# Second attention: weighing with the value slices stationary in four column groups

## The chip, the core and the metric

The kernel runs on one core of a Trainium2 chip. The metric is device time in microseconds (us) of one execution. The core has TensorE (PE: matmuls, with weight loads shown apart as PEld), VectorE (DVE), ScalarE (ACT), GpSimd (POOL) and SyncE (SP), each with its own queue, which it works through in order.

## What is computed

32 batches of 128 tokens with 128 features go through four parts, each added to its input: an attention of 16 heads of 8, a mixture of 8 experts (two for each token, with a capacity), a second attention of 16 heads of 64, and a mixture of 16 experts (one for each token) beside a shared one. The change lies in the second attention:

```python
q = (x @ w_q).reshape(B, SQ, N_HEADS, D_HEAD)        # 16 heads of 64
k = (cond @ w_k).reshape(B, SKV, N_HEADS, D_HEAD)
v = (cond @ w_v).reshape(B, SKV, N_HEADS, D_HEAD)
attn = jnp.einsum('bqhd,bkhd->bhqk', q, k) * scale
attn = jax.nn.softmax(attn, axis=-1)
out = jnp.einsum('bhqk,bkhd->bqhd', attn, v).reshape(B, SQ, N_HEADS * D_HEAD)
return out @ w_out + b_out
```

## The kernel before

One batch of 128 queries and 128 keys is one step of the second attention; `attention` in the TensorE block writes the order of a step by hand, and the blocks of the other engines have the same loop `for b in range(1, LAST)` (30 steps, b = 1 to 30) with their parts. What is in flight is of several batches: step b has the scores of b, the coarse product (for the row maxima) and the values of b+1, the keys of b+2, and the weighing and output of b-1.

- Scores (`score_half`, L1077) come out with the keys on the partitions; ScalarE's `exponential` (L1471) writes them as `pT` (f32, keys x queries). VectorE's `high_half` (L1779) copies them to bf16 `ph`, GpSimd's `low_halves` (L713) makes the bf16 rest `pl`. The values have the same two parts, `va1` high (ScalarE, `take_values`, L1464) and low (VectorE, `low_values`, L1793). A product of the two is so three or four bf16 matmuls.
- Weighing (`weigh(b, g)`, L1115) does four heads, a group g of 0 to 3, into the one PSUM bank `of`. For each head it has four matmuls with `ph` or `pl` stationary (128x128) and `va1` moving: 64 columns of values and a 65th of ones (zeros in the low part), which gives the sum of the weights. The result has the queries on the partitions.
- `evacuate(b, g)` (VectorE, L1769) takes the reciprocal of the four sums (128x4) and multiplies the 256 columns by it into `o1`. It increments `pv_free`, for which the next `weigh` waits, as `of` is single.
- The output projection needs the features on the partitions. `fill("oT0")` and `fill("oT1")` (L1019) transpose `o1` in four pieces each, through the identity, into a PSUM bank; ScalarE's `take` (L1440) copies it to `oT`; `fill("y")` multiplies its eight pieces with `wo1` (L1018).
- A step of TensorE is: scores half 0, coarse half 0, weigh(b-1, 2), queries q1 and q0 (L1027), oT0, weigh(b-1, 3), scores half 1, coarse half 1, weigh(b, 0), oT1, values (L1073), weigh(b, 1), `turn` (four small transposes and the router's product), y, keys (L1053).
- A step of VectorE is: maximum of coarse half 0 (`half_max`, L1786), evacuate(b-1, 2), high_half(b, 0), statistics of a later batch, evacuate(b-1, 3), maximum of half 1, evacuate(b, 0), high_half(b, 1), a normalisation, low values, evacuate(b, 1), `add_output`, statistics, every fourth step `choose_expert` and another fourth `keep_ranks`, `combine` and a normalisation.
- `drain` does the last batch and mixes it with the shared expert.

The step of TensorE in the code:

```python
                    for b in range(1, LAST):
                        score_half(b, 0)
                        coarse_half(b + 1, 0)
                        weigh(b - 1, 2)
                        fill("q1", b + 1)
                        ...
                        fill("oT0", b - 1)
                        weigh(b - 1, 3)
                        score_half(b, 1)
                        coarse_half(b + 1, 1)
                        weigh(b, 0)
                        fill("oT1", b - 1)
                        values_of(b + 1)
```

## Time and profile before

| | |
|---|---|
| runs, median | 958.36 us (952.79 to 963.0, 3 runs) |
| span of the profiled execution, first to last instruction | 894.0 us |
| PE busy in the span | 836.1 us (94%) |
| DVE busy | 577.2 us (65%) |
| ACT busy | 537.0 us (60%) |
| POOL busy | 450.6 us (50%) |
| mean granted TensorE clock | 0.979 |

The page has no other duration for the profiled execution than its span; the 64.4 us between it and the median of the runs lie outside the first and last instruction. The second attention lies between about 315 and 756 us of the span. A busy PE is not a PE at its peak, as matmuls overlap each other in the records; the chain of waits tells better which piece of work followed which.

### The profile page before, as it was taken

The numbers are of one execution on the slowest core, as the hardware profiler recorded it, in microseconds if no ns is written. First come the engines' busy times: TensorE is split into PE (matmuls) and PEld (weight loads), VectorE is DVE, ScalarE is ACT, GpSimd is POOL, SyncE is SP. The second block draws the span as 40 slices with busy tenths as digits, with TensorE's granted clock in tenths as the row PEclk, the third lists the DMA queues.
The fourth block names the chain that finished last, engine by engine and source line by source line (L and its number), as shares of the span: only waits on it lengthen the run. The fifth ranks groups of instructions, "written<-read, shape, count | busy, mean of one in ns | idle before, by whom it ended". The sixth has DMA issues, their size and how long they took to land.

```text
span 894.0 us, 30924 instructions
## 1 busy us (share of the span) xinstructions
PE 836.1 (94%) x12318; PEld 711.1 (80%) x12318; DVE 577.2 (65%) x1613; ACT 537.0 (60%) x1132; POOL 450.6 (50%) x544
## 2 busy tenths in 40 slices
PE   6999999788899989999999999999999998899994
PEld 3566666543899869999999999999999997797994
DVE  5788888842124367777777777777777675644662
ACT  3788888541566656666666656657667653225772
POOL 7123444466013136556556566575574443673664
PEclk7899999999999999999999999999999999999997
DMA  5333432211665235641010010110110000345440
GB/s 155 111 111 109 130 118 81 80 34 52 188 193 152 78 103 159 195 145 32 18 32 26 23 33 20 29 32 20 30 32 11 21 3 1 98 146 160 129 123 8
DMA packets 75215, 71.98 MB, mean 81 GB/s; under 512 B 13409, under 2 KB 66984, under 8 KB 74306
## 3 DMA queue, kind: packets, MB, share of 16 engines
q1 hardware_dynamic: 67138, 55.05, 21.0%
q0 software_dynamic: 7136, 14.71, 5.2%
q8 instruction: 101, 1.65, 0.8%
q10 hardware_dynamic: 800, 0.24, 0.1%
q14 instruction: 40, 0.33, 0.1%
HBM read 37.72 MB, written 30.49 MB: 76 GB/s over the span
## 4 chain that ended last, share of the span: by engine, by line
PE 76%; DVE 8%; issue 7%; POOL 4%; ACT 2%; DMA 2%; SPq 0%; POOLq 0%; DVEq 0%; ACTq 0%
PE of L1124 8%; PE sf L1088 8%; PE jf L1018 6%; PE sf L1073 5%; PE mf L1053 5%; PE sf L1299 4%; PE sf L1289 4%; PE jf L1027 4%; PE sf L1027 3%; PE sf L1210 3%; PE sf L1330 2%; PE sf L851 2%; POOL out L796 2%; PE mf L1111 2%; PE of L897 2%
## 5 line engine op out<-in xcount | busy, mean ns | idle before, releaser
L720 POOL TENSOR_TENSOR pl<-pT,ph 128x512 bf16<-128x512 f32 x128 | 146.0, 1164 | 132.4 <-DVE ph L1784 131.9
L1790 DVE TENSOR_REDUCE cmxb<-mf 128x8 bf16<-128x1024 f32 x64 | 78.3, 1224 | 57.4 <-PE mf L1111 57.4
L664 POOL DMA_INDIRECT buf<-gu,slots x64 | 63.7, 995 | 64.8 <-PE of L897 46.2
L1632 DVE TENSOR_REDUCE cmx<-mf 128x8 bf16<-128x1024 f32 x64 | 78.3, 1224 | 24.2 <-PE mf L878 23.7
L1476 ACT ACTIVATE pT<-sf 128x1024 f32<-128x1024 f32 x64 | 66.9, 1045 | 25.1 <-PE sf L1094 25.1
L1088 PE MATMUL sf<-qTs,kTs 64*128 64x128 f32 x1024 | 74.4, 285 | 0.1
L709 POOL DMA_INDIRECT gb<-eo,slots x56 | 57.6, 1029 | 26.3 <-DMA eo<-rows 13.4
L1394 ACT ACTIVATE pTf<-sf 128x1024 f32<-128x1024 f32 x64 | 62.5, 1019 | 10.0 <-PE sf L858 9.7
L1088 PEld LDWEIGHTS sf<-qTs,kTs 64*128 64x128 f32 x1024 | 62.2, 187 | 5.8 <-issue 0.3
L1457 ACT CAST kTb<-mf 128x512 bf16<-128x512 f32 x30 | 17.6, 585 | 81.2 <-PE sf L1053 81.2
L2045 DVE TENSOR_TENSOR rows<-sf,dn 128x256 f32<-128x256 f32 x40 | 17.0, 425 | 72.2 <-PE sf L1299 71.8
L796 POOL DMA_INDIRECT out<-rows x47 | 45.6, 970 | 32.0 <-issue 18.9
L1018 PE MATMUL jf<-wo,oT 128*128 128x128 f32 x480 | 60.7, 280 | 0.0
L1775 DVE TENSOR_TENSOR o1s<-of,rden 128x256 f32<-128x256 f32 x128 | 54.4, 425 | 4.4
L1018 PEld LDWEIGHTS jf<-wo,oT 128*128 128x128 f32 x480 | 56.0, 192 | 0.0
L1073 PE MATMUL sf<-wv,ctxT 32*128 32x256 f32 x768 | 51.8, 400 | 2.5 <-DVE va10l L1799 2.5
L1053 PE MATMUL sf<-ctxT,wk 32*128 32x128 f32 x768 | 51.4, 278 | 1.1 <-ACT qTs L1447 0.7
L1330 PE MATMUL sf<-xsT,qTs 128*128 128x128 f32 x376 | 49.6, 275 | 0.0
L1053 PE MATMUL mf<-ctxT,wk 32*128 32x128 f32 x720 | 48.2, 279 | 0.0
L1053 PEld LDWEIGHTS sf<-ctxT,wk 32*128 32x128 f32 x768 | 45.3, 186 | 1.5 <-issue 0.8
L1784 DVE CAST ph<-pT 128x1024 bf16<-128x1024 f32 x64 | 44.1, 689 | 3.1 <-ACT pT L1476 3.1
L1330 PEld LDWEIGHTS sf<-xsT,qTs 128*128 128x128 f32 x376 | 45.7, 192 | 0.0
(284 smaller groups left out, 2609.3 us busy)
## 6 DMA issues: line engine op xcount, KB each, us to landing
buf<-zero SPq DMA_DIRECT2D x12, 516.0 KB, 7.4
ctxT<-in_ctxP SPq DMA_DIRECT2D x32, 192.0 KB, 2.8
rows<-buf SPq DMA_DIRECT2D x47, 129.0 KB, 2.1
buf<-zero SPq DMA_DIRECT2D x20, 256.0 KB, 3.5
rows<-buf SPq DMA_DIRECT2D x40, 128.0 KB, 2.3
eo<-rows SPq DMA_DIRECT2D x40, 128.0 KB, 2.3
gu<-in_gu SPq DMA_DIRECT2D x4, 1024.0 KB, 7.0
rows<-in_x SPq DMA_DIRECT2D x8, 256.0 KB, 5.1
```

Of the source, the lines that this page charges most:

```text
L664: nc.gpsimd.indirect_dma_start(out=buf0[:, :], out_offset=bass.IndirectOffsetOnAxis(ap=slots0[:, k, b:b + 1], axis=0), in_=xna0[:, b, :], ...
L720: nc.gpsimd.tensor_tensor(pl[h][:, :, c, :], pT[h][:, :, c, :], ph[h][:, :, c, :], ALU.subtract)\
L796: nc.gpsimd.indirect_dma_start(out=out_rows, out_offset=bass.IndirectOffsetOnAxis(ap=xs1[n % XRING][:, ID:ID + 1].bitcast(I32), axis=0), i ...
L1018: last = nc.tensor.matmul(ps[:, 0:DM], oT[:, c, :], wo1[:, c, :], start=(c == 0), stop=(c == NCH - 1))
L1053: last = nc.tensor.matmul(banks[i][:, c * P:(c + 1) * P], wk1[rr, u, c * P:(c + 1) * P], ctxT[n % 2][rr, u, :], start=(u == 0), stop=(u == ...
L1073: last = nc.tensor.matmul(sf[:, i, 0:UC], ctxT[n % 2][rr, u, :], wv1[rr, u, :], start=(u == 0), stop=(u == CB - 1))
L1088: nc.tensor.matmul(S1[:, r, n * P:(n + 1) * P], kT[p][rr, 4 * h + n, :], qT[p][rr, 4 * h + n, :], start=(n == 0), stop=False)
L1124: last = nc.tensor.matmul(of[:, j * (D1 + 1):(j + 1) * (D1 + 1)], pp[h][:, r, n, :], va1[p][part][:, QH * g + j, :], start=(m == 0), stop= ...
L1330: last = nc.tensor.matmul(g_bank[n % DEEP][:, c * P:(c + 1) * P], stage[n % DEEP][:, c * P:(c + 1) * P], xsT1[n % DEEP], start=True, stop= ...
L1476: nc.scalar.activation(pT[h][:, :, :, :].rearrange("p r c n -> p r (c n)"), S1, ACT.Exp, scale=D1 ** -0.5)\
L1632: nc.vector.reduce_max(to, mf[:, :, :].rearrange("p c (j k) -> p c j k", j=QH), AX.X)\
L1790: nc.vector.reduce_max(cmx1[b % 2][:, :].rearrange("p (r k) -> p r k", r=2)[:, :, 4 * h:4 * h + 4], M1p[:, :, :].rearrange("p r (c k) -> p ...
```

## The change

The operands of the weighing change places. The values are now stationary, in slices of 32 columns, and the weights `ph` and `pl` are moving with their 128 columns. The four heads of a group lie in four column groups of the array: head j writes partitions 32j to 32j+31 of `of`. Slice u of 0 and 1 fills columns 128u to 128u+127. The sums come from a stationary slice of ones, with `ph` and `pl` moving, in columns 256 to 383: each sum stands on all 32 partitions of its head. The result has the features on the partitions, so `o1`, the transposes `oT0` and `oT1` and their copies by ScalarE go, `evacuate` writes `oT` (now double) itself, and the rows of `wo1` are put in the order head group, slice, head on the host. A group has 40 matmuls where it had 16. `va1` loses its 65th column and the four memsets of it. Some waits are renamed for it (`values_of` waits for `k_free` where it waited for the copy of oT0; constants that count the memsets fall by four). `xrn` and `ctxT` are declared in another place.

```diff
@@ step_fills, bank_for
-        order = [("q1", b + 1), ("q0", b + 2), ("oT0", b - 1), ("oT1", b - 1), ("y", b - 1)]
+        order = [("q1", b + 1), ("q0", b + 2), ("y", b - 1)]
...
-        va1 = [[sb(f"va1{p}{n}", [P, NH, D1 + 1], BF16) for n in "hl"] for p in range(2)]
-        rden = sb("rden", [P, QH])
+        va1 = [[sb(f"va1{p}{n}", [P, NH, D1], BF16) for n in "hl"] for p in range(2)]
+        rden = sb("rden", [P, P])
...
-        oT = sb("oT", [P, NCH, P])
+        oT = [sb(f"oT{p}", [P, NCH, P]) for p in range(2)]
...
@@ fill, TensorE
                     if name == "y":
-                        L1.free(pe, "oT0", n)
-                        L1.free(pe, "oT1", n)
+                        pe.wait_ge(L1.pv_free, 4 * n + 4)
                         for c in range(NCH):
-                            last = nc.tensor.matmul(ps[:, 0:DM], oT[:, c, :], wo1[:, c, :], start=(c == 0), stop=(c == NCH - 1))
-                    elif what == "oT":
-                        pe.wait_ge(L1.pv_free, 4 * n + 2 * h + 2)
-                        for c in range(4):
-                            last = nc.tensor.transpose(ps[:, c * P:(c + 1) * P],
-                                                       o1[p][:, 8 * h + 2 * c:8 * h + 2 * c + 2, :], ident[:, :])
+                            last = nc.tensor.matmul(ps[:, 0:DM], oT[p][:, c, :], wo1[:, c, :], start=(c == 0), stop=(c == NCH - 1))
...
@@ values_of, TensorE
                         pe.wait_ge(L1.exp_done, 2 * n)
-                        L1.free(pe, "oT0", n - 2)
+                        pe.wait_ge(L1.k_free, 2 * n + 2)
...
@@ weigh, TensorE
-                    for j in range(QH):
-                        n, r = 2 * (g % 2) + j // 2, j % 2
+                    def product(cols, weights, of_p, first, final):
+
+                        for j in range(QH):
+                            n, r = 2 * (g % 2) + j // 2, j % 2
+                            last = nc.tensor.matmul(of[32 * j:32 * j + 32, cols], weights(QH * g + j), of_p[h][:, r, n, :],
+                                                    start=first, stop=final)
+                        return last
+
+                    for u in range(2):
                         for m, (pp, part) in enumerate(((ph, 0), (ph, 1), (pl, 0), (pl, 1))):
-                            last = nc.tensor.matmul(of[:, j * (D1 + 1):(j + 1) * (D1 + 1)], pp[h][:, r, n, :],
-                                                    va1[p][part][:, QH * g + j, :], start=(m == 0), stop=(m == 3))
+                            product(slice(u * P, (u + 1) * P), lambda k: va1[p][part][:, k, 32 * u:32 * u + 32], pp,
+                                    u == 0 and m == 0, False)
+                    product(slice(2 * P, 3 * P), lambda k: ones[:, 0:32], ph, False, False)
+                    last = product(slice(2 * P, 3 * P), lambda k: ones[:, 0:32], pl, False, True)
                     last.then_inc(L1.pv_full, 1)
...
@@ evacuate, VectorE
-                    ov = of[:, 0:QH * (D1 + 1)].rearrange("p (h d) -> p h d", d=D1 + 1)
-                    nc.vector.reciprocal(rden[:, :], ov[:, :, D1]).then_inc(L1.rden_done, 1)
+                    nc.vector.reciprocal(rden[:, :], of[:, 2 * P:3 * P]).then_inc(L1.rden_done, 1)
                     dve.wait_ge(L1.rden_done, 4 * b + g + 1)
-                    nc.vector.tensor_tensor(o1[b % 2][:, QH * g:QH * (g + 1), :], ov[:, :, 0:D1],
-                                            rden[:, :].unsqueeze(2).broadcast_to([P, QH, D1]), ALU.mult)\
+                    nc.vector.tensor_tensor(oT[b % 2][:, 2 * g:2 * g + 2, :],
+                                            of[:, 0:2 * P].rearrange("p (u n) -> p u n", u=2),
+                                            rden[:, :].unsqueeze(1).broadcast_to([P, 2, P]), ALU.mult)\
                         .then_inc(L1.pv_free, 1)
...
-        "wo1": lay(np.asarray(L1_xattn_w_out).reshape(NCH, P, DM).transpose(1, 0, 2)),
+        "wo1": lay(np.asarray(L1_xattn_w_out).reshape(NQ, QH, 2, 32, DM).transpose(1, 3, 0, 2, 4).reshape(P, NCH, DM)),
```

## Rows read from the trace of the kernel before

**Rows 1.** The page's first part: busy time, share of the span, instructions.
```profile
PE 836.1 (94%) x12318; PEld 711.1 (80%) x12318; DVE 577.2 (65%) x1613; ACT 537.0 (60%) x1132; POOL 450.6 (50%) x544
```

**Rows 2.** The chain of waits, one step: start us, length us, what.
```profile
495.92 0.33 PE mf L1111 x8
496.24 0.59 PE of L1124 x16
496.83 0.97 PE jf L1027 x8
...
498.70 0.44 PE sf L1022 x4
499.13 0.48 PE of L1124 x16
...
501.16 0.59 PE of L1124 x16
501.75 0.47 PE jf L1022 x4
502.22 1.51 PE sf L1073 x24
503.72 0.59 PE of L1124 x16
504.73 1.88 PE jf L1018 x16
...
509.47 0.32 PE mf L1111 x8
```

**Rows 3.** Timeline of VectorE, same step: start, length, engine, line, idle before.
```profile
496.28 1.22 DVE L1790 TENSOR_REDUCE cmxb<-mf 128x8 bf16<-128x1024 f32 x1 [1.17 <-PE mf L1111]
497.42 0.17 DVE L1773 RECIPROCAL rden<-of 128x4 f32<-128x4 f32 x1
497.62 0.42 DVE L1775 TENSOR_TENSOR o1s<-of,rden 128x256 f32<-128x256 f32 x1
497.97 0.68 DVE L1784 CAST ph<-pT 128x1024 bf16<-128x1024 f32 x1
...
499.65 0.18 DVE L1773 RECIPROCAL rden<-of 128x4 f32<-128x4 f32 x1 [0.40 <-PE of L1124]
...
501.19 1.23 DVE L1790 TENSOR_REDUCE cmxb<-mf 128x8 bf16<-128x1024 f32 x1 [0.90 <-PE mf L1111]
502.34 0.17 DVE L1773 RECIPROCAL rden<-of 128x4 f32<-128x4 f32 x1
...
504.41 1.29 DVE L1799 TENSOR_TENSOR va10l<-sf,va10h 128x512 bf16<-128x512 f32 x2 [0.54 <-ACT va10h L1468]
...
506.64 0.29 DVE L1883 TENSOR_TENSOR rows<-rows,jf 128x128 f32<-128x128 f32 x1 [0.39 <-PE jf L1018]
...
509.83 1.23 DVE L1790 TENSOR_REDUCE cmxb<-mf 128x8 bf16<-128x1024 f32 x1 [0.18 <-PE mf L1111]
```

**Rows 4.** Timeline of TensorE, first attention: f32 column groups, bf16 row groups.
```profile
99.89 1.08 PE L897 MATMUL of<-pTf,vq 128*32 128x128 f32 x32
...
103.43 0.40 PE L858 MATMUL sf<-cT,sel 4*128 4x128 bf16 x16
```

**Rows 5.** Timeline of TensorE in the drain: matmuls of 16 columns.
```profile
760.80 0.24 PE L1271 MATMUL jf<-selq,ones 128*128 128x16 bf16 x4
760.90 0.17 PE L1272 MATMUL jf<-selsum,ones 128*128 128x16 bf16 x1
```

**Rows 6.** Single lines, all of the span: reciprocals on VectorE, min/median/max ns, shape.
```profile
L1773 DVE RECIPROCAL rden<-of x128: 172/174/185, 329.0 to 750.7; 128x4 f32<-128x4 f32 x128
L1734 DVE RECIPROCAL rdenf<-jf x32: 247/248/258, 35.9 to 195.9; 128x16 f32<-128x16 f32 x32
L2015 DVE RECIPROCAL rows<-v x1: 356/356/356, 763.9 to 763.9; 128x32 f32<-128x32 f32 x1
```

**Rows 7.** Timelines of TensorE and VectorE in `drain`.
```profile
744.95 2.02 PE L1018 MATMUL sf<-wo,oT 128*128 128x128 f32 x16 [1.23 <-ACT oT L1449]
...
742.37 0.70 DVE L1784 CAST ph<-pT 128x1024 bf16<-128x1024 f32 x1 [1.76 <-ACT pT L1476]
```

More of the change, by code:

```diff
@@ L145, in bank_for @@
     if b >= LAST:
-        return {"oT0": 0, "oT1": 2, "y": 0}[name]
+        return 0
     if (name, n) == ("q0", 2):
@@ L150, in bank_for @@
         return 1
-    return {"q0": 0, "q1": 2, "oT0": 1, "oT1": 2, "y": 2}[name]
+    return {"q0": 0, "q1": 2, "y": 2}[name]
 def moved_at(b):
@@ L272, in build @@
         veA, rsA, veF, rstd = [sb(n, [P, NB]) for n in ("veA", "rsA", "veF", "rstd")]
-        xrn = [sb(f"xrn{p}", [DM, P]) for p in range(2)]
         wq0 = sb("wq0", [DM, DM])
@@ L283, in build @@
         xnT = [sb(f"xnT{p}", [DM, P]) for p in range(2)]
-        ctxT = [sb(f"ctxT{p}", [P, CB, P]) for p in range(2)]
-        va1 = [[sb(f"va1{p}{n}", [P, NH, D1 + 1], BF16) for n in "hl"] for p in range(2)]
-        rden = sb("rden", [P, QH])
+        va1 = [[sb(f"va1{p}{n}", [P, NH, D1], BF16) for n in "hl"] for p in range(2)]
+        rden = sb("rden", [P, P])
         with ExitStack() as front_only:
@@ L312, in build @@
         pl = [sb(f"pl{h}", [P, 2, QH, P], BF16) for h in range(2)]
-        o1s = sb("o1s", [P, 2 * NH, D1])
-        o1 = [o1s[:, p * NH:(p + 1) * NH, :] for p in range(2)]
-        oT = sb("oT", [P, NCH, P])
+        oT = [sb(f"oT{p}", [P, NCH, P]) for p in range(2)]
+        xrn = [sb(f"xrn{p}", [DM, P]) for p in range(2)]
+        ctxT = [sb(f"ctxT{p}", [P, CB, P]) for p in range(2)]
         hT = [sb(f"hT{p}", [P, 2, 2 * P]) for p in range(2)]
@@ L614, in _ @@
                     nc.gpsimd.memset(vq[p][:, :, :, D0:D0 + 1], 1.0).then_inc(const_done, 1)
-                for p in range(2):
-                    for part in range(2):
-                        nc.gpsimd.memset(va1[p][part][:, :, D1:D1 + 1], 1.0 - part).then_inc(const_done, 1)
                 pool.wait_ge(mask_loaded, 16)
@@ L1188, in attention @@
                             fill("q0", b + 2)
-                        fill("oT0", b - 1)
                         weigh(b - 1, 3)
@@ L1193, in attention @@
                         weigh(b, 0)
-                        fill("oT1", b - 1)
                         values_of(b + 1)
@@ L1230, in drain @@
                     score_half(LAST, 1)
-                    fill("oT0", LAST - 1)
-                    fill("oT1", LAST - 1)
                     weigh(LAST, 0)
@@ L1242, in drain @@
                     shared_gate(2)
-                    fill("oT0", LAST)
-                    fill("oT1", LAST)
                     shared_down(1)
@@ L1522, in attention @@
                             take("q0", b + 2)
-                        take("oT0", b - 1)
                         exponential(b, 1)
-                        take("oT1", b - 1)
                         take_values(b + 1)
@@ L1542, in drain @@
                     nc.scalar.activation(table[:, :], mhalf[:, 0:1], ACT.Silu)
-                    take("oT0", LAST - 1)
-                    take("oT1", LAST - 1)
                     shared_gate(0)
@@ L1548, in drain @@
                     shared_gate(2)
-                    take("oT0", LAST)
-                    take("oT1", LAST)
                     shared_gate(3)
```

27 lines of the change are left out of this document (11 added, 16 removed).

## The prediction

> **What bounds the kernel now.** The change lies in the second attention, so I looked first at how the page shares out the span (TensorE is busy for 94% of it [rows 1]) and then at the chain of waits inside one step of that attention [rows 2]. The reader is to see there that one piece of TensorE work follows the other without a gap: from the start of one coarse product (495.92) to that of the next (509.47) is 13.55 us, one batch, and every piece between is TensorE's. 30 such steps (b = 1 to 30) are the loop. So today TensorE sets the pace. The third view is VectorE's own order of work in the same step [rows 3]: it waits 0.40, 0.90, 0.54 (for ScalarE), 0.39 and 0.18 us, up to and with the wait before the next step's maximum. VectorE is close behind TensorE: 2.4 us in 13.6 are free in this step, which has `keep_ranks`; the 1.17 us before its first maximum shows that a step without it has about 1 us more.
>
> In offsets from the start of the coarse product (C = 0), which I use below, the pieces of [rows 2] start at: weighing of group 2 (W2) 0.32, transposes oT0 2.78, W3 3.21, W0 5.24, oT1 5.83, values 6.30, W1 7.80, output product y 8.81, next C 13.55. VectorE's, from [rows 3]: maximum D1 0.36, evacuation of group 2 1.50, bf16 copy 2.05, evacuation of group 3 3.73, maximum D6 5.27, evacuation of group 0 6.42, low part of the values 8.49, `add_output` 10.72, next D1 13.91.
>
> **The change, part by part.**
>
> *Transposes.* The two pieces oT0 (0.44) and oT1 (0.47) leave TensorE: -0.91 us per step [rows 2]. The two ScalarE copies behind them go too; they are worth nothing by themselves, for ScalarE is not in the chain.
>
> *Weighing on TensorE.* Before, 16 matmuls of 65 columns take 0.48 us, or 0.59 where the piece before used another division of the array [rows 2]; so such a change of division costs 0.11. After, a group has 40 matmuls: 2 slices x 4 products x 4 heads, and 2 x 4 for the sums, each with 32 stationary and 128 moving columns, four neighbours in four column groups. Before has no bf16 matmul of this shape. From below: the bf16 matmuls that lie in four row groups, L858, start (0.40 - 0.213)/15 = 12.5 ns apart, and the first attention's f32 products in four column groups, L897, start (1.08 - 0.273)/31 = 26 ns apart [rows 4]. An f32 record streams at half the speed of bf16 (L1018 needs 1.88/16 = 117 ns for 128 columns, the bf16 L1124 0.48/16 = 30 ns for 65 [rows 2]), so L897 halved is 13 ns, and both rows agree: 40 x 0.014 = 0.56 us, +0.08 over 0.48. From above: 25 ns each, as for the four 16-column products from 760.80 to 760.90 [rows 5], is 1.00 us. I take 0.56, since L858 is bf16 and L897 has the very shape, but both are short bursts (16 and 32), and 40 in a row behind a wait have no row. The weighing is now the only 128x32 work, so three borders more change the division (W2 to q1, q0 to W3, W1 to turn): +0.33 per step. TensorE alone: -0.91 + 4 x 0.08 + 0.33 = -0.26 us per step.
>
> *A rule that speaks against 0.56.* The Trainium skill, "TensorE: Matmul & The Clock Gate", section "The HAM clock gate", says that matmuls never start less than about 25 ns apart, however small they are. By that, 40 of them would be 1.0 us and not 0.56; L858's 12.5 ns [rows 4] disagrees for a burst of 16, and no row here shows a longer one. "TensorEngine Tiling (Array Packing)", section "Restrictions and Gotchas", adds that column tiling excludes the fast weight load.
>
> *The reciprocal on VectorE.* This is the term that decides. The sums now come out as 128x128 (every head's sum repeated on its 32 partitions), and the reciprocal is taken of all of it instead of 128x4. Its duration grows with the columns: 174 ns at 4, 248 at 16, 356 at 32 [rows 6]; that is 6.2 and 6.75 ns a column, 6.5 over all. At 128 columns: 174 + 124 x 6.5 = 0.98 us, bounds 0.94 (slope 6.2) to 1.01 (slope 6.75). So each evacuation grows by 0.80 us, and VectorE by 4 x 0.80 = 3.2 us a step, against 2.4 to 3.4 free. The multiplication behind it keeps its 256 columns and its 0.42 us [rows 3].
>
> *A rule on it.* "VectorE: DVE Perf Modes" of the Trainium skill, section "Walkthrough: the 8-slice pipeline in each mode", says that the reciprocal repeats its divide 8 times; at the page's 0.96 GHz that is 8.3 ns a column. By the page one reciprocal would be 1.21 us; the rows' 6.5 ns a column disagree.
>
> *Where it lands.* The bank `of` is single, so W3 waits for the evacuation of group 2, W0 for that of 3, W1 for that of 0. VectorE goes through them in a fixed order. From D1 at 0.36: evacuation of 2 starts 1.50, VectorE free 0.55 + 0.80 later at 2.85; copy and statistics 1.28 (from 497.97 to 499.65 without the 0.40 waited) -> 4.13. W3: 0.32 + 0.67 + 0.11 + 1.87 (q1 and q0, from 496.83 to 498.70) = 2.97, no wait to speak of (the evacuation is done at 1.50 + 0.62 + 0.80 = 2.92); over at 3.64. So evacuation of 3 starts at 4.14 (VectorE is late, not TensorE, against 3.73 before), VectorE free 5.49, result at 5.56; W0 starts 5.66 with 0.1 for TensorE to see it (before 5.24; TensorE alone 3.64 + 1.55 = 5.19, 1.55 being from W3's end to W0 in [rows 2]). D6 5.49 to 6.64 (1.15 as from 501.19 to 502.34). Evacuation of 0: 6.64, result 8.06; W1 8.16 (before 7.80; TensorE alone 5.19 + 0.67 + 1.51 = 7.37). Here is the new wait of the chain: about 0.8 us before W1, and 0.5 before W0. Behind W1 stand turn, y, the keys of b+2, the next scores and the next coarse product, all in TensorE's order: W1 over 8.83 with its entry, +0.11 -> 8.94 against 8.39 before: **+0.55 us**. From there all is as before up to the next C, 14.10.
>
> Does VectorE then keep up on the second half? Free at 7.99; copy and normalisation 0.98 (502.89 to 503.87) -> 8.97; low values 1.2 -> 10.2; evacuation of 1 -> 11.5; from `add_output` to the next D1 3.01 (506.64 to 509.65) -> 14.5, against 13.91 + 0.55 = 14.46 needed. Just met. `choose_expert` has two small operations more than `keep_ranks`, each no shorter than the 0.17 of [rows 3], so one step in four is late by about 0.4: +0.1 on the mean. Together **+0.65 us a step**, x 30 = +19.5.
>
> *Before and behind the loop.* In step 0 W(0,1) waits for the first evacuation, and the keys behind it: +0.7. In `drain` six evacuations follow one another, each 0.8 longer. Against that stand the waits for ScalarE's copies of oT before y, such as 1.23 us at 744.95, and VectorE's own of 1.76 us at 742.37 [rows 7], all gone or free; I set the sum at 0, +-2. The four memsets on GpSimd that go are hidden in its wait for the first statistics. The weights `wo1` are only laid out otherwise on the host, with the same bytes; no transfer moves.
>
> *The sum.* Span 894.0 + 19.5 + 0.7 = 914.2 us; what lies around the span in the median of 958.36 (64.4 us) stays: **979 us**.
>
> **The rivals.**
>
> A. *The forecast*: VectorE's long reciprocals pace the loop, weighing 0.56. 979 us; own range 970 to 990: a reciprocal of 0.94 or 1.01 moves the three evacuations in the loop by 3 x 0.04 x 30 = 4 us either way, drain 2, the small-step lateness (0 to 0.2 a step) 3. Chance 0.60.
>
> B. *Weighing at 25 ns a matmul* (the floor of [rows 5]). Each weighing +0.44 over A. W3 ends at 0.32 + 1.11 + 0.11 + 1.86 + 1.11 = 4.51, evacuation of 3 starts 4.55, W0 6.07, evacuation of 0 7.23, W1 8.75, turn 9.97 against 8.39: +1.58 a step, +47, and 1.5 outside: 1007 us. For it: 40 pairs in a row behind a wait have no row; against it: 12.5 ns of L858. The page quoted on the 25 ns would have this. Chance 0.24.
>
> C. *The other side: VectorE's growth is covered and TensorE alone counts.* W1 waits for nothing if the evacuation of group 0 is done at 7.37. By the walk it is done, with TensorE's 0.1 to see it, at 5.76 + 3x, x being the growth of one reciprocal; so x must be under 0.53, a 128x128 reciprocal under 0.70 us, or 4.2 ns a column where the rows have 6.5. Then -0.26 x 30 = -8: 950 us, not slower. A milder form is that orders overlap better than my walk has them, down to +0.1 or 0.2 a step, the saturation of VectorE alone (3.2 against 2.4 to 3.4 free): about 963. Both together 0.12.
>
> D. *The column groups don't overlap for bf16*: 40 x 0.055 = 2.2 us a weighing, about +6.5 a step, 1150 us. Against it L897 with its 26 ns. 0.02. And a reciprocal of 1.21 us (by the page): 3 x 0.23 a step, 1000 us, 0.02.
>
> **How the numbers follow.** The likeliest is A, 979. The range goes from 962 (the milder form of C) to 1015 (B and what its bounds add); it leaves out the stronger C, D and the tails, some 0.15. Faster by over 1% (under 948.8) needs more than all of TensorE's saving: 0.05. Within 1% (about what a measurement of this kernel can tell from no change): C for the rest, 0.11. Slower by over 1%: A, B, D, 0.84.
>
> **What would show it.** Right: the reciprocal of 128x128 at 0.94 to 1.01 us, VectorE near 13.5 us busy a step, a step of 14.1 to 14.3 us, the chain of waits passing through VectorE (reciprocal, multiplication) into W0 and W1, 40 weighing matmuls in 0.56 us. TensorE's busy share falls there. Wrong: weighing pieces of 1 us (then B), no VectorE in the chain (then C), a granted clock below 1.0 in the loop, which TensorE's pauses of 0.5 to 0.8 us should not bring and which nothing in my sum holds.

## The result

The changed kernel is slower: **1007.46 us** (1006.14 to 1012.36, 4 runs) against 959.15 us of the kernel before in the same comparison, a ratio of 1.0521 (95% interval 1.047 to 1.0572). The forecast had 979 us: +20 us, where +48 us came.

One fact is needed to read all that follows. The kernel before takes about 900 us on some chips and 959 to 968 us on others: in the experiments below two chips were of the first kind, one of them in two groups of runs, and two of the second. In every execution whose time and span are both known the time is 1.7 to 1.9 us longer than the span. So the profiled execution of the kernel before (span 894.0) took about 896 us and must have been on a chip of the first kind; its timed runs and those of the changed kernel were on one of the second. I call them here chips of 900 and of 960, after the time of the kernel before. Every ratio is of one chip; where a difference is taken across two, the text says so.

| | before, chip of 900 | changed, chip of 960 | changed, chip of 900 |
|---|---|---|---|
| median | 900.65 | 1007.46 | 931.42 |
| ratio to before on the same chip | 1 | 1.0521 | 1.0352 (1.0289 to 1.0415) |
| span of the profiled execution | 894.0 | 1005.2 | 931.0 |
| VectorE's coarse maximum of one step to that of the next, mean of the 30 steps | 13.54 | 15.20 | 14.48 |
| the same, mean of steps 10 to 25 | 13.58 | 15.02 | 14.20 |

The page of the changed kernel in the compared run (busy time with its share; the instruction queue; the shares of the chain that ended last; the costliest group of VectorE):

```profile
PE 876.2 (87%) x15134; PEld 720.6 (72%) x15134; DVE 666.1 (66%) x1613; ACT 502.7 (50%) x1068; POOL 447.0 (44%) x540
...
q8 instruction: 123, 2.02, 0.8%
...
PE 50%; DVE 23%; issue 18%; ACT 2%; POOL 2%; another core or an unknown queue 2%; DMA 1%; SPq 1%; DVEq 0%; ACTq 0%; POOLq 0%
...
L1753 DVE RECIPROCAL rden<-of 128x128 f32<-128x128 f32 x128 | 121.4, 948 | 15.0 <-PE of L1112 10.6
```

Against [rows 1] (a chip of 900), TensorE falls from 94% to 87% of the span and VectorE has 88.9 us more. The reciprocals' own durations grow by 128 x (0.948 - 0.174) = 99 us; records that follow each other without a pause overlap by up to 0.1 us, which the busy time counts once, and more of them do so now. VectorE has 23% of the chain.

Inside a step, three views tell the story. First the chain of waits on a chip of 900 (start us, length us, what), which answers to [rows 2]:

```profile
491.12 0.29 PE mf L1098 x8
491.42 0.67 PE of L1112 x40
...
494.15 0.74 PE of L1112 x40
...
496.47 1.23 DVE cmxb L1771
497.69 0.87 DVE rden L1753
...
498.59 0.43 DVE oT L1755
...
499.16 0.74 PE of L1112 x40
...
500.42 1.89 PE jf L1010 x16
```

From the coarse product at 491.12 (C = 0), weighing of group 2 starts at 0.30, of group 3 at 3.03, of group 1 at 8.04, the output product y at 9.30. The wait that the change makes is the one before 8.04: TensorE stands until VectorE's maximum, reciprocal and multiplication of group 0 are through. VectorE is busy for 13.60 of the 14.19 us from 491.45 to 505.64. This step has `choose_expert` and is VectorE's fullest; in the steps before and behind it VectorE is busy for 12.45 of 14.45 and 12.62 of 14.40 us.

Second, the same chain of the compared run, on a chip of 960:

```profile
531.97 0.74 PE of L1112 x40
532.72 2.90 PE sf L1060 x24
535.64 0.59 ACT va10h L1455
536.25 1.29 DVE va10l L1780 x2
537.54 0.87 DVE rden L1753
...
542.15 1.13 DVE cmxb L1771
```

Here the values have a piece of 2.90 us, 1.51 in [rows 2], and all of VectorE's work up to the next step's maximum hangs on it: the step from 526.75 to 542.07 is 15.32 us, though VectorE is busy for 13.65 of them, as on the other chip.

Third, the timeline around these values:

```profile
532.69 1.58 PE L1060 MATMUL sf<-wv,ctxT 32*128 32x256 f32 x24
532.83 0.99 POOL L704 DMA_INDIRECT gb<-eo,slots  x1 [0.16 <-issue]
534.13 0.96 POOL L704 DMA_INDIRECT gb<-eo,slots  x1 [0.30 <-issue]
535.57 0.30 PE L1112 MATMUL of<-pl,va11l 128*32 128x128 bf16 x4 [0.44 <-issue]
535.64 0.58 ACT L1455 CAST va10h<-sf 128x512 bf16<-128x512 f32 x1 [3.05 <-PE sf L1060]
```

The matmuls themselves are no longer (1.58 us). But ScalarE starts to read 2.95 us behind their start, and TensorE's own weighing stands 0.44 us before its 29th matmul, which starts at 535.57. Both go on together, 0.5 us after GpSimd's second indirect gather (two a step, which fetch the expert outputs for batch b+6, L704) has ended. In the settled steps of this run ScalarE starts 2.64 to 2.98 us behind the values. On chips of 900 it is 1.63 to 1.65 us in nearly all steps of every kernel measured, also with the two gathers beside them as here. The granted clock of the settled steps is 1.00 on chips of both kinds, so it is not what tells them apart.

### The profile page after: what moved, and what is told of

It reads as the page before. It is cut to its first block, busy times and chain, and to the rows that moved or that the text cites. A ratio compares the mean times of both kernels' runs of the same rounds, so it can differ in the third digit from the quotient of the medians.

```text
span 1005.2 us, 36424 instructions
## 1 busy us (share of the span) xinstructions
PE 876.2 (87%) x15134; PEld 720.6 (72%) x15134; DVE 666.1 (66%) x1613; ACT 502.7 (50%) x1068; POOL 447.0 (44%) x540
## 3 DMA queue, kind: packets, MB, share of 16 engines
q8 instruction: 123, 2.02, 0.8%
## 4 chain that ended last, share of the span: by engine, by line
PE 50%; DVE 23%; issue 18%; ACT 2%; POOL 2%; another core or an unknown queue 2%; DMA 1%; SPq 1%; DVEq 0%; ACTq 0%; POOLq 0%
DVE rden L1753 6%; PE of L1112 6%; DVE cmxb L1771 5%; PE sf L1075 5%; PE sf L1320 4%; PE jf L1010 4%; PE sf L1289 4%; PE sf L1279 3%; PE sf L1060 3%; PE mf L1040 3%; DVE oT L1755 2%; DVE va10l L1780 1%; PE sf L1204 1%; PE mf L1098 1%
## 5 line engine op out<-in xcount | busy, mean ns | idle before, releaser
L1753 DVE RECIPROCAL rden<-of 128x128 f32<-128x128 f32 x128 | 121.4, 948 | 15.0 <-PE of L1112 10.6
L1384 ACT ACTIVATE pTf<-sf 128x1024 f32<-128x1024 f32 x64 | 62.5, 1020 | 27.2 <-remote 17.2
L704 POOL DMA_INDIRECT gb<-eo,slots x56 | 54.7, 976 | 26.3 <-DMA eo<-rows 13.4
L1060 PE MATMUL sf<-wv,ctxT 32*128 32x256 f32 x768 | 53.8, 400 | 6.3 <-DVE va10l L1780 5.3
L1755 DVE TENSOR_TENSOR oT<-of,rden 128x256 f32<-128x256 f32 x128 | 54.3, 424 | 4.4
L1040 PE MATMUL sf<-ctxT,wk 32*128 32x128 f32 x768 | 51.4, 278 | 1.1 <-ACT qTs L1436 0.7
L2053 DVE TENSOR_TENSOR hT<-kTs,sf 128x256 f32<-128x256 f32 x47 | 19.8, 421 | 45.5 <-ACT kTs L1586 24.3
L892 PE MATMUL of<-pTf,vq 128*32 128x128 f32 x1024 | 41.5, 295 | 8.0 <-ACT oh L1398 5.0
L1060 PEld LDWEIGHTS sf<-wv,ctxT 32*128 32x128 f32 x768 | 40.1, 188 | 11.5 <-issue 8.0
```

The lines of the kernel that those rows point to most:

```text
L1040: last = nc.tensor.matmul(banks[i][:, c * P:(c + 1) * P], wk1[rr, u, c * P:(c + 1) * P], ctxT[n % 2][rr, u, :], start=(u == 0), stop=(u == ...
L1060: last = nc.tensor.matmul(sf[:, i, 0:UC], ctxT[n % 2][rr, u, :], wv1[rr, u, :], start=(u == 0), stop=(u == CB - 1))
L1753: nc.vector.reciprocal(rden[:, :], of[:, 2 * P:3 * P]).then_inc(L1.rden_done, 1)
L1755: nc.vector.tensor_tensor(oT[b % 2][:, 2 * g:2 * g + 2, :], of[:, 0:2 * P].rearrange("p (u n) -> p u n", u=2), rden[:, :].unsqueeze(1).bro ...
```

## The experiments

In all of them a step is the time from VectorE's coarse maximum in one step to the same in the next. What they gave, with the two chips apart ("values seen": start of the values to ScalarE's first read; steps are counted from the one that starts in step b = 0 of the code). The i kernels ran once and have no interval; f4_before_late ran twice, in 956.38 and 971.31 us, and its profile is of the longer one. The times that the expectations name are counted from 959 us for the kernel before, also where the runs then fell on a chip of 900.

| kernel | chip (before) | time | ratio (95%) | steps 2 to 5 | mean of steps 10 to 25 | values seen |
|---|---|---|---|---|---|---|
| before | 900 | 900.18 | 1 | 53.7 | 13.58 | 1.65 |
| e2_long | 900.18 | 918.92 | 1.0212 (1.0175 to 1.0249) | 55.4 | 14.13 | 1.65 |
| g3_long | 900.65 | 920.68 | 1.0249 (1.0193 to 1.0305) | 55.4 | 14.13 | 1.65 |
| e1_short | 900.18 | 908.18 | 1.0095 (1.0057 to 1.0132) | 64.7 | 13.70 | 1.63 |
| e4_both | 900.18 | 914.77 | 1.0154 (1.0103 to 1.0206) | 68.9 | 13.71 | 1.64 |
| e3_between | 900.18 | 930.81 | 1.0353 (1.0303 to 1.0402) | 68.4 | 14.28 | 1.64 |
| g4_after | 900.65 | 931.42 | 1.0352 (1.0289 to 1.0415) | 66.4 | 14.20 | 1.64 |
| g1_moved | 900.65 | 927.5 | 1.0347 (1.0277 to 1.0417) | 64.3 | 14.26 | 1.64 |
| g2_plain | 900.65 | 930.9 | 1.037 (1.0309 to 1.043) | 65.9 | 14.26 | 1.64 |
| f1_after | 966.17 | 1015.99 | 1.0549 (1.0472 to 1.0627) | 69.9 | 15.10 | 3.0 |
| f2_late | 966.17 | 1013.19 | 1.0509 (1.0432 to 1.0586) | 59.1 | 15.10 | 3.0 |
| f3_short_late | 966.17 | 1011.43 | 1.0491 (1.04 to 1.0581) | 60.6 | 15.19 | 2.6 |
| f4_before_late | 966.17 | 956.38, 971.31 | | 54.4 | 13.70 | 2.4 |
| i1_plain | 968.45 | 995.36 | | 68.4 | 14.34 | 1.64 |
| i2_late | 968.45 | 1013.99 | | 59.1 | 15.09 | 3.0 |
| i3_moved | 968.45 | 1025.21 | | 67.3 | 15.44 | 1.64 |

### The reciprocal and the weighing apart

e1_short keeps the new weighing and takes the long reciprocal away (the sums are not used, so the division is left out); e2_long does the reverse, the kernel before with a reciprocal over 128 columns. e3_between puts a matmul over the whole array between the weighing of group 0 and the values, where oT1 was, and e4_both is e1_short with it.

```diff
 e1_short
-  nc.vector.reciprocal(rden[:, :], of[:, 2 * P:3 * P]).then_inc(L1.rden_done, 1)
+  nc.vector.reciprocal(rden[:, 0:QH], of[:, 2 * P:2 * P + QH]).then_inc(L1.rden_done, 1)
 e2_long
-  nc.vector.reciprocal(rden[:, :], ov[:, :, D1]).then_inc(L1.rden_done, 1)
+  nc.vector.reciprocal(rden[:, :, :], ov[:, :, D1 - 31:D1 + 1]).then_inc(L1.rden_done, 1)
 e3_between
+  need(pe, L1.pj_free[2], FILL1["y", b - 1][1])
+  nc.tensor.matmul(jf[:, 0:P], identb[:, :], identb[:, :], start=True, stop=True)
```

> The changed kernel with the reciprocal taken of 4 columns again; the other columns of rden are a constant, so the division by the sums is left out of the result. The profile of the changed kernel shows two things beside the forecast: the reciprocals of 0.95 us, and values pieces (the 24 matmuls of L1060) that TensorE's chain holds for 2.9 us where they took 1.51. Theory 1 (the slow values are TensorE's own affair: they come straight behind a weighing in four column groups, another division of the array): the reciprocals go, the slow values stay, -0.26 + 1.3 us a step in 30 steps: about 990 us, values still 2.9 us from start to ScalarE. Theory 2 (the slow values come of the reciprocals on VectorE, which overlap them, or of TensorE's waits for these): values back to 1.6 us, TensorE alone counts, about 951 us.

> The kernel before with only the reciprocal made long: 128 columns (32 of each head, the sum the last of them) where it took 4; the result is the same. By the walk of the prediction with TensorE's pieces of before, W1 comes at 8.23 in place of 7.80 and choose_expert adds 0.1: +0.5 us a step, 975 us. If the long reciprocals alone make the values slow (theory 2), 975 plus up to 1.3 us a step: 1007 to 1015 us, as the whole change. If VectorE's growth is covered: 959 us.

> The changed kernel with one bf16 matmul of 128x128 on 128 columns put between weigh(b, 0) and the values, so that they no longer follow the column groups directly. Theory 1: values back to 1.6 us from start to ScalarE, and the time near the forecast, 980 to 988 us. Theory 2, or another cause in the values themselves: values stay at 2.9 us, 1007 to 1012 us.

> Both edits: reciprocal of 4 columns (the division left out) and the matmul between. What is left of the change is TensorE's: transposes gone, 40 weighing matmuls a group, three more borders. The forecast's -0.26 us a step: 951 to 955 us by either theory. Over 970 us: TensorE's part of the change costs of itself, and weighing is slower than 13 ns a matmul in truth.

The long reciprocal alone costs 18.7 us (ratio 1.0212), and its steps settle at 14.01 to 14.14 us, with every fourth at 14.34 to 14.45. That is VectorE's new pace with the TensorE of before, and it is the forecast's mechanism by itself. Its page has the same duration as the changed kernel:

```profile
L1773 DVE RECIPROCAL rden<-of 128x128 f32<-128x128 f32 x128 | 121.5, 949 | 2.9 <-PE of L1124 2.6
```

The new weighing alone does not gain: ratio 1.0095, interval above 1. Two things hold it back. In the settled steps the 0.91 us of the transposes comes back as other work. The chain of e1_short from the values of one step to those of the next:

```profile
486.69 1.58 PE sf L1060 x24
488.26 0.67 PE of L1112 x40
488.94 0.16 PE mf L1137
...
495.20 1.09 PE jf L1014 x8
...
500.06 0.29 issue
500.35 0.67 PE sf L1060 x5
```

Four weighings of 0.67 are 2.68 us where [rows 2] has 0.59 + 0.48 + 0.59 + 0.59 = 2.25 (+0.43); q1 is 1.09 and not 0.97 (+0.12), the values 1.58 and not 1.51 (+0.07). The first piece of `turn`, behind W1, is 0.16 where the chain of the kernel before has

```profile
504.31 0.06 PE mf L1141
```

(+0.10). With -0.91 that is -0.19 us. And right before the values stand 0.29 us in which TensorE waits: since oT1 no longer lies there, the values come up before ScalarE's exponential of half 1 has freed the bank they write to. That this is the wait is read from the code (`values_of` waits for `exp_done`), and e4_both bears it out. It puts one more matmul there, and the wait is shorter by just its length, the values starting 0.1 us behind the exponential's end (493.82 + 1.02) as in e1_short:

```profile
493.82 1.02 ACT L1465 ACTIVATE pT<-sf 128x1024 f32<-128x1024 f32 x1 [0.85 <-PE sf L1081]
494.65 0.16 PE jf L1190
494.81 0.13 issue
```

The sum is +0.10; measured are +0.12 us a step.

The second thing is in the first steps: steps 2 to 5 take 64.7 us, ten more than four settled ones. It is taken up below.

e3_between and e4_both put a wide piece back in front of the values: 14.28 against 14.20 us a step, 13.71 against 13.70. So the order "weighing, then values" is not what costs. They were also to tell whether it is what makes ScalarE see the values late, but on this chip nothing is late.

### Late signals on chips of 960

f1_after is the changed kernel as it is. f2_late issues SyncE's background transfers (weights for later stages) behind the loop and not beside it; f3_short_late is e1_short with that, f4_before_late the kernel before with that.

```diff
 f2_late (SyncE)
                         ctx_batch(b + 1)
+                for b in range(-1, NB):
                     background(b)
```

> The changed kernel once more, beside the same runs of the kernel before as the three that follow. The first profile of it had two costs above the forecast's step: values pieces that ScalarE saw done only after 2.9 us, with a pause of 0.7 us inside weigh(b, 1), and slow first steps (16.5 to 19 us). In the runs with one edit the first is absent and the second is there. Theory S (supply: TensorE now runs 346 pairs of load and matmul a step in place of 250, and where the DMA queues are busy its instructions come late): slow first steps again, 12 to 16 us in all; the slow values come and go with the run, so the ratio is 1.035 to 1.052. Theory M (the slow values belong to the change, the matmul between cured them): ratio 1.050 to 1.055, steps of 14.9 us.

> The changed kernel with the background transfers of steps 2 to 7 (expert weights gu, wgu, wdn and the zeros for buf1) issued by SyncE only after the last step of the second attention. Theory S: no first step over 14.6 us, the loop 12 to 14 us shorter than in the changed kernel, and no pause of TensorE with issue as its cause over 0.5 us inside a weighing. If the slow first steps come of the change's own waits: the loop is as long as before this edit. The time behind the loop grows by what the transfers take there, so the steps decide, not the total.

> The reciprocal of 4 columns (the division by the sums left out of the result) and the background transfers after the loop. What is left in the loop is TensorE's part of the change alone. Theory S: all steps 13.6 to 13.8 us, none over 14. Otherwise first steps of 14.7 to 19.5 us as with the short reciprocal alone.

> The kernel before with the background transfers after the loop, for what that edit does by itself. Its first steps have no pauses to lose, so the steps stay at 13.2 to 13.6 us by theory S; the time behind the loop grows as in the other two. If its loop shortens as much as theirs, the transfers cost something that has nothing to do with the number of TensorE's instructions.

With the background transfers gone the values are still seen after 3.0 us and the step stays at 15.1. So these transfers are not the cause. What does end it is the gathers' end: the last steps have none, since there is no batch b+6 any more, and in them (27 to 29) the changed kernel takes 14.06, 14.07 and 14.2 us in the compared run, as on a chip of 900, and the values are seen after 1.63. The kernel before has the effect too (values seen after 2.30 to 2.67 us in f4_before_late), but its steps are 13.70 us, 0.12 more than on a chip of 900: VectorE has the free time of [rows 3] to wait for the values.

f3_short_late shows that VectorE's free time is not all. It has the short reciprocal, VectorE is busy for only 9.69 us of the step of 15.30 that starts at 564.64, and 13.6 to 13.8 us a step were expected; yet its settled steps take 15.19. Another signal is late there:

```profile
569.91 0.23 PE L1113 MATMUL of<-pl,ones 128*32 128x128 bf16 x4
571.19 0.96 POOL L705 DMA_INDIRECT gb<-eo,slots  x1 [0.30 <-issue]
572.78 0.18 DVE L1754 RECIPROCAL rden<-of 128x4 f32<-128x4 f32 x1 [2.05 <-remote]
573.57 0.24 PE L1113 MATMUL of<-ph,va10h 128*32 128x128 bf16 x4 [0.90 <-DVE oT L1756]
```

The weighing of group 0 is over at 570.14, VectorE's maximum before it at 570.73, and the reciprocal that waits for that weighing starts at 572.78, 0.6 us behind the second gather; W1 waits for it. Where this signal comes earlier (every fourth step, 14.62 to 14.70 us) or there are no gathers (13.67), the step is shorter. In f4_before_late the reciprocal of group 0 follows the maximum (552.55 + 1.23) without a pause, at 553.69, though the first gather starts at 552.89 there; why the signal is not held in that order is not shown. So what a late signal costs depends on which one it is, and the new weighing alone is enough for a step of 15.2 us on such a chip. The long reciprocal alone (e2_long) ran on chips of 900 only, so how the loss divides between the two is open.

Whether the gathers do it or only end at that moment needs them moved or taken away. g1_moved puts them behind `low_halves(b, 1)`, g2_plain replaces those of t >= 7 by plain transfers of the same size on SyncE's queue. g3_long and g4_after are e2_long and the changed kernel again.

```diff
 g1_moved, h2_moved, i3_moved (GpSimd)
                             bias(b + 3)
-                        if inside(b + 6):
-                            fetch(b + 6)
                         if inside(b):
                             low_halves(b, 1)
+                        if inside(b + 6):
+                            fetch(b + 6)
 g2_plain, h1_plain, i1_plain (SyncE; the fetch on GpSimd goes)
+                        for k in range(2):
+                            sp.dma_start(gb[t % 4 * 2 + k][:, :], eo0[t * P:(t + 1) * P, :]).then_inc(x_in[2 * (t % 4) + k], 16)
```

> The changed kernel with GpSimd's two gathers of the expert rows (fetch(b + 6)) moved behind low_halves(b, 1), some 3 us later in the step. Where a run of the changed kernel is slow in every step (14.9 to 15.0 us), VectorE, ScalarE and SyncE see TensorE's signals only about 0.65 us after the second gather has ended. Theory G (while GpSimd issues its indirect transfers, TensorE's completion signals are held back): ScalarE sees the values again 1.64 us after their start, and steps fall to 14.1 to 14.4 us, less what is held back at the new place (the output product, the keys). Theory O (the late signals have another cause): steps of 14.9 us and 3.0 us from the values to ScalarE, wherever the gathers stand.

> The changed kernel with the gathers of batches 7 to 31 replaced by plain transfers of as many bytes (64 KB each, fixed rows of eo0 and so wrong values) from SyncE's queue; GpSimd issues none in the loop. Theory G: no late signal anywhere, steps of 14.05 to 14.2 us from b = 7 on, as in the last steps of the changed kernel, which have no gather; ratio to before about 1.03. Theory O: 14.9 us.

> The kernel before with the reciprocal of 128 columns, once more: this is the reciprocals' share beside the same runs of before as the other three. The first such run had 14.0 to 14.1 us a step and a ratio of 1.021. Theory G: where signals are held back by gathers (before and long reciprocals have them as well), 14.2 to 14.9 us a step, as the gathers come later against the values. Theory O, or a chip that holds none back: 14.0 to 14.1 us and 1.02.

> The changed kernel once more, as the reference of these runs. If the chip holds signals back: ratio 1.050 to 1.055, steps of 14.9 us. If it does not: steps of 14.05 to 14.2 us from b = 7 on, ratio about 1.035, the forecast's loop (+0.5 to 0.65 us a step) and the slow first steps.

These four fell on a chip of 900, where the changed kernel has its 14.2 us with the gathers where they were, moved or gone (14.20, 14.26, 14.26). They tell that the gathers cost nothing there, and give the changed kernel's ratio on such a chip, 1.0352. The three of the next group, one run each, fell on one too (before 896.16 in the one run beside them): 934.13, 928.55 and 931.2 us, settled steps of 14.18, 14.25 and 14.20. "Embedding rows" in the expectations are the expert outputs of L704.

> The changed kernel with GpSimd's gathers of the embedding rows (from the second of them on, t >= 7) replaced by plain transfers of the same size from SyncE's queue (other rows, so the output differs). Theory 'the gathers hold TensorE's signals back': on a chip where the kernel before takes about 960 us, ScalarE's first read of the values falls from 3.0 to about 1.65 us behind their start, as in the last five steps without gathers, and a step from 15.0 to 14.1 us: about -0.9 us in some 24 steps, -20 us against h3_after. Rival 'it is the traffic of these bytes, or the chip itself': still 3.0 us and 15.0 us a step. On a chip of the faster kind (before 900 us): 1.65 us and 14.1 us in both kernels, nothing told apart.

> The changed kernel with GpSimd's fetch(b+6) (two gathers) behind low_halves(b,1) and not ahead of it, some 4 us later in the step. Theory 'the gathers hold the signals back': on a chip of the slower kind the values are seen after 1.65 us, and another signal, near the new place of the gathers, is late by up to 1.4 us instead; the step is 14.1 to 14.8 us according to whether that one is in the chain. Rival 'the chip itself': the values stay at 3.0 us, the step at 15.0.

> The changed kernel unaltered, the reference on the same chip for h1_plain and h2_moved. On a chip of the slower kind: values seen after 3.0 us, step 15.0 us with gathers and 14.1 us in the last five without, about 1010 us. On one of the faster kind: 1.65 us, 14.1 us and about 931 us.

The last group, one run each, fell on a chip of 960:

> The changed kernel with GpSimd's gathers of the embedding rows replaced by plain transfers of the same size from SyncE's queue (other rows, so the output differs). On a chip where before takes about 960 us: if the gathers hold TensorE's signals back, ScalarE reads the values 1.65 us behind their start instead of 3.0 and a step takes 14.1 us instead of 15.0; if it is the traffic or the chip itself, 3.0 and 15.0 stay. On one where before takes 900 us: 1.65 and 14.1, as with the gathers.

> The changed kernel with SyncE's background transfers (weights for later stages) issued behind the loop over the batches. Theory 'TensorE's instructions come late while bulk transfers run': on a chip where before takes 900 us, steps 1 to 5 of the second attention fall from about 80 us together to about 72 (14.1 to 14.6 each), and TensorE's pauses of 2 to 3.3 us without a cause are gone from them; the total hardly gains, since the transfers then land behind the loop. Rival 'the first steps are slow by their own order (first gathers, expert work)': they stay at 17, 15, 18 and 15 us. On a chip of the slower kind: as f2_late, 14.6 to 14.9 us from the second step.

> The changed kernel with GpSimd's fetch(b+6) behind low_halves(b,1). On a chip where before takes about 960 us: if the gathers hold the signals back, the values are seen after 1.65 us and another signal near the new place is late; else 3.0 us and 15.0 us a step stay. On one where before takes 900 us: 14.1 us a step, as the changed kernel.

i1_plain, with the bytes moved by SyncE's queue: steps 6 to 25 of 14.07 to 14.76 us but for one (15.2), values seen after 1.64, 995.36 us, which is 18.6 less than i2_late and 29.9 less than i3_moved beside it. Its timeline, TensorE's products and ScalarE's first read of each:

```profile
538.60 1.58 PE L1063 MATMUL sf<-wv,ctxT 32*128 32x256 f32 x24
...
540.25 1.07 ACT L1458 CAST va11h<-sf 128x512 bf16<-128x512 f32 x2 [1.98 <-PE sf L1063]
540.62 0.91 SPq L589 DMA_DIRECT2D gb<-eo  x2
...
543.48 0.38 PE L1043 MATMUL mf<-ctxT,wk 32*128 32x128 f32 x2
...
545.16 0.58 ACT L1447 CAST kTb<-mf 128x512 bf16<-128x512 f32 x1 [2.82 <-PE sf L1043]
```

i3_moved has the gathers beside the keys (L1040) and not beside the values (L1060):

```profile
525.71 1.88 PE L1060 MATMUL sf<-wv,ctxT 32*128 32x256 f32 x24
...
527.64 1.07 ACT L1455 CAST va11h<-sf 128x512 bf16<-128x512 f32 x2 [2.03 <-PE sf L1060]
...
530.48 0.99 POOL L704 DMA_INDIRECT gb<-eo,slots  x1 [0.17 <-issue]
530.59 0.38 PE L1040 MATMUL mf<-ctxT,wk 32*128 32x128 f32 x2
...
531.78 0.95 POOL L704 DMA_INDIRECT gb<-eo,slots  x1 [0.30 <-issue]
...
533.55 0.59 ACT L1444 CAST kTb<-mf 128x512 bf16<-128x512 f32 x1 [4.22 <-PE sf L1040]
```

The lateness has moved with them. The values are seen after 1.63 to 1.93 us. The keys are seen 2.96 us behind their start, where i1_plain and f1_after have 1.69; again the release is 0.8 us behind the end of the second gather. The keys lie in TensorE's own path (the next scores and the coarse product need them), and the step is longer still: 15.44 us, 1025.21 in all. Taking the gathers away and moving them both did what the theory asks, and the last steps of every run on such a chip, which have no gathers, agree; so on chips of 960 GpSimd's indirect gathers hold back what TensorE signals. (The plain transfers are issued 2 us behind the start of the values, not beside them, so they show that no signal in the step's path is late with them, not what they would do at the gathers' place.) What in such a chip is different is not known; the same kernel with the gathers in the same place beside the keys has 1.69 us on a chip of 900 (h2_moved).

### The first steps

Steps 2 to 5 take 53.7 us in the kernel before and 64 to 70 in every kernel with the new weighing and the background transfers beside it, on both chips; e2_long and g3_long, which have the long reciprocal but TensorE's work of before, take 55.4. So it is TensorE's new work and not VectorE's. e1_short shows what happens. Timeline of its TensorE, the pauses alone:

```profile
338.34 1.01 PE L1014 MATMUL sf<-xrn,wq 128*128 128x128 f32 x3 [3.34 <-issue]
...
356.95 0.23 PE L1112 MATMUL of<-pl,ones 128*32 128x128 bf16 x3 [0.89 <-issue]
...
369.91 0.23 PE L1112 MATMUL of<-pl,va10h 128*32 128x128 bf16 x1 [2.20 <-issue]
```

These are pauses for which the profile has no releaser, two of them in the middle of a weighing, where no semaphore is waited for. And the stretches (span, busy time and instructions of each engine, granted clock, share of the DMA engines, GB/s), of e1_short:

```profile
330.00:340.00 10.00, 6.66 (x134) 6.07 (x132) 3.42 (x9) 4.09 (x8) 3.81 (x5) 0.89 0.63 205
338.30:344.50 6.20, 6.16 (x88) 5.48 (x92) 0.61 (x2) 1.47 (x3) 2.05 (x3) 0.50 0.09 24
```

and of the kernel before:

```profile
330.00:340.00 10.00, 10.00 (x207) 9.29 (x209) 6.24 (x15) 7.68 (x14) 3.42 (x4) 1.00 0.59 203
```

Under the same traffic of 203 to 205 GB/s the old TensorE is never idle and the new one stands for a third of the time. Behind the pause of 3.34 us the granted clock is 0.50, the level of 1.2 GHz, for 6.2 us, which costs about 3.1 us more (an estimate: half of 6.2). With a fourth pause of 0.57 us at 386.29 the pauses make 7.0 us; with the clock that is 10.1, and the four steps took 9.9 us more than four settled ones. f2_late and i2_late take the traffic away: steps 2 to 5 are 59.1 us, against 69.9 of f1_after, that is 10.8 us less and no more than four settled steps there (60.4). So the loss in these steps needs both, the new weighing and the bulk transfers. Step 1 is another matter: it takes 16.47 us in f2_late, where no first step over 14.6 was expected, and 12.81 in i2_late, and it goes from 11.9 to 17.2 us among all runs with the new weighing; its spread is not explained. The likely link is the supply of instructions: a step has about 340 pairs of weight load and matmul where it had about 250 ((15134 - 12318) / 32 = 88 more: 96 for the weighing, less the eight transposes, which the 346 of the expectations forgets), and the page's instruction queue carries more, 2.02 MB above and in the kernel before

```profile
q8 instruction: 101, 1.65, 0.8%
```

That link was argued, not shown: no run changed the number of instructions alone. The 10.8 us are hardly seen in the total (1013.19 against 1015.99), since the transfers now land behind the loop, where the last step takes 19.07 us against 14.29.

## Why the prediction was right in its direction and short by 28 us

**The step that failed** is the sum. It priced the change by VectorE's wait alone, +0.65 us in each of 30 steps, and put two things at nothing: that the first steps might take longer than TensorE's pieces add up to (its instructions coming late is the likely link, not shown), and that the other engines might see TensorE's signals more than the walk's 0.1 us late. In the compared run the first is 14 us and the second 17 us (below). That the measured 1007 us lies inside the range up to 1015 is luck: the upper part of the range was put there for rival B, which did not occur.

**The loop was right.** Forecast were 14.10 us for a step and, with the steps of `choose_expert`, +0.65 on the mean. Where no signal is late the settled step is 14.20 against 13.58, **+0.62** (30 steps: 18.6 of the 19.5 us). The walk holds place by place: W3 at 3.03 (forecast 2.97), W0 at 5.56 (5.66), W1 at 8.04 (8.16), y at 9.30 (8.81 + 0.55 = 9.36). The wait came where it was put, before W1. VectorE is busy 13.60 us in the fullest step and 13.0 on the mean from 470 to 700 us of g4_after (forecast near 13.5): "just met" holds for the steps with `choose_expert`, not for all.

**The terms.** The reciprocal is 0.947 us (forecast 0.98, lower bound 0.94), the slope 6.2 ns a column from 4 to 128. The Trainium skill, "VectorE: DVE Perf Modes", section "Walkthrough: the 8-slice pipeline in each mode", has the divide repeated 8 times, from which an estimate of 1.21 us was worked out: the measurement disagrees. The 40 matmuls of a weighing start from first to tenth group of four in

```profile
531.97 0.24 PE L1112 MATMUL of<-ph,va11h 128*32 128x128 bf16 x4 [0.25 <-DVE oT L1755]
...
532.47 0.24 PE L1112 MATMUL of<-pl,ones 128*32 128x128 bf16 x4
```

0.50 us, 14 ns each, so the 12.5 to 13 ns of the short bursts [rows 4] carried to 40 in a row, and the 0.56 was right. The Trainium skill, "TensorE: Matmul & The Clock Gate", section "The HAM clock gate", states a floor of 25 ns from start to start: this trace disagrees for matmuls in column groups. A change of the array's division cost 0.12 us at q1 and 0.10 at `turn`, as forecast (0.11). TensorE's work by itself came out at -0.19 (forecast -0.26).

**Rival B** gives 1007 us, which is what was measured, by accident: its mechanism, 25 ns a matmul, did not occur. (The chances given for over 1% slower, 0.84, do not agree with those of A, B and D, which make 0.88.) **Rival C** could not have come about even with a short reciprocal: e1_short has that, and is at 1.0095. The step that failed in it is "TensorE alone": the forecast counted the durations of TensorE's pieces and let them follow one another, but the transposes had covered ScalarE's exponential, and without them the values wait 0.29 us for it.

**What the sum lacked.** Two terms, and a false one:

1. *The first steps.* To add up TensorE's pieces by their durations leaves out that the instructions must arrive. On chips of 900 the first five steps take 78.9 us against 66.8, of which 3.1 are the forecast's: **9 us missing**; in the compared run 84.3, 14 us missing (3.4 of them in step 1, which took 17.22 us there and 12.54 in g4_after; that spread is unexplained). The prediction named a granted clock below 1.0 in the loop as what nothing in its sum holds. It came, in e1_short for 6.2 us, but behind a pause and not by itself.
2. *GpSimd's gathers on chips of 960*: 15.02 against 14.20 us in some 21 steps, **17 us missing**. i1_plain shows that it is theirs. The kernel before has a late signal too and pays 0.12 us a step. In the step of the compared run shown above, which has `choose_expert`, the changed kernel pays because VectorE has no time left: low values, evacuation of 1 and the work up to the next maximum all move back by what the values are late. But f3_short_late, with 5 us of VectorE free, pays more (15.19 us a step against e1_short's 13.70 on a chip of 900), through the signal of the weighing of group 0. So a full VectorE accounts for that step and is not the whole cause.
3. *"What lies around the span (64.4 us) stays"* was false: nothing of the kind lies there. The compared run has a span of 1005.2 us and a time of 1007.07. The 64 us were the difference between two chips. It did not shift the forecast's difference, but it hid that the profile read was of a chip without term 2.

The sum for the compared run, in the 30 steps, is 18.6 + 14 + 17 = 50 us. Measured are 456.0 - 406.3 = 49.7 against the kernel before on a chip of 900, 456.0 - 409.8 = 46.2 against f4_before_late on one of 960 (which has no background transfers beside it), and 48.3 in the whole time. On a chip of 900: 18.6 + 9 = 27.6; measured 434.4 - 406.3 = 28.1, and 30.8 in the medians. That leaves 2.7 us before and behind the loop, at the edge of the forecast's +0.7 and 0 +-2; one execution cannot tell this better, for the first coarse maximum alone comes at 317.0 us in g4_after and at 312.0 in h3_after, the same kernel.

## What to carry to other kernels

A signal that comes late costs nothing or more than a microsecond a step, according to which piece waits for it: a change that fills an engine, or only moves a piece against the others, can turn the one into the other. When a piece is taken from the engine that sets the pace, look for what it covered (here an exponential) before its time is booked as a gain. And cost many short instructions twice, by their duration and by whether they come in time while bulk transfers run; and before a span is set against a median, see whether both are of the same chip.

## What the runs showed of the hardware

- Chips differ: the kernel before takes 900 us on some and 959 to 968 on others, and the difference is not one factor. In the changed kernel the first coarse maximum of the second attention is at 312.0 and 317.0 us of the span on the one kind (h3_after, g4_after) and at 340.0 and 341.9 on the other (after, f1_after). The settled steps of the kernel before are 13.58 us on the one and 13.70 on the other (f4_before_late), all at a granted clock of 1.00.
- On chips of 960 GpSimd's indirect gathers hold back TensorE's signals until mostly 0.5 to 0.8 us behind the second gather (2.6 to 3.05 us instead of 1.65 for the values in `after` and f3_short_late, about 3.0 instead of 1.69 for the keys in i3_moved), and TensorE's own matmuls stand meanwhile (0.44 us in `after`). With plain transfers of the same bytes, issued 2 us behind the start of the values, nothing in the step's path was late (i1_plain).
- bf16 matmuls of 128x32 in four column groups start 14 ns apart, 40 in a row behind a wait.
- A reciprocal of 128x128 takes 947 ns, of 128x4 174 ns.
- TensorE can stand for up to 3.3 us without any wait in the profile while transfers run at 205 GB/s, and behind that pause its granted clock was 0.50 (1.2 GHz) for 6.2 us (e1_short).
